# A fused attention and feed-forward kernel: another opening order for its first loads and weights, and other PSUM banks at its end

## The reference

```python
xn = layernorm(x)                                    # over channels, eps 1e-5
q, k, v = (xn @ qkv_w + qkv_b), split into heads
q, k = l2norm(q), l2norm(k)
kv = einsum('bhnd,bhne->bhde', k, v)                 # linear attention: no softmax
att = einsum('bhnd,bhde->bhne', q, kv) @ proj_w + proj_b
ffn = relu(xn @ W1 + b1) @ W2 + b2                   # 1024 inner columns
out = x + att + ffn
```

## Time and profile before

| what | value |
|---|---|
| median of three runs | 557.03 us |
| the profiled execution: its own time | 557.46 us |
| its span, first to last instruction | 555.7 us |
| PE busy | 550.4 us, 99% of the span, 2724 instructions |
| DVE, ACT, POOL busy | 412.8, 285.1, 117.9 us |
| granted TensorE clock | 1.00 in every one of the 40 slices |
| chain that ended last | PE 89%, ACT 3%, DVE 3%, DMA 2% |

### The profile page before, as it was taken

How to read it: one execution, slowest core, us unless ns; L and a number is a source line. 1 busy time by engine, 2 the same in 40 slices (tenths; PEclk the granted TensorE clock), 3 DMA queues, 4 the chain that set the end, 5 groups by cost and what they waited for, 6 DMA issues and landing times.

```text
span 555.7 us, 8968 instructions
## 1 busy us (share of the span) xinstructions
PE 550.4 (99%) x2724; PEld 467.3 (84%) x2724; DVE 412.8 (74%) x802; ACT 285.1 (51%) x518; POOL 117.9 (21%) x148
## 2 busy tenths in 40 slices
PE   9999999999999999999999999999999999999997
PEld 7788888888888888888888888888888888888896
DVE  6897899676795967859677686876778777783755
ACT  4675564656436563365644556455554555533421
POOL 3242424302052020520213202331024301150100
PEclk9999999999999999999999999999999999999999
DMA  8432134343503434134341343414333251313412
GB/s 259 159 87 49 34 83 95 84 103 86 106 14 86 97 87 95 21 85 98 86 87 28 90 95 85 80 37 112 71 94 65 45 106 38 84 32 81 107 39 77
DMA packets 141414, 45.36 MB, mean 82 GB/s; under 512 B 133330, under 2 KB 136402, under 8 KB 141396
## 3 DMA queue, kind: packets, MB, share of 16 engines
q1 hardware_dynamic: 139280, 44.61, 34.8%
q10 hardware_dynamic: 2116, 0.53, 0.5%
HBM read 20.98 MB, written 8.39 MB: 53 GB/s over the span
## 4 chain that ended last, share of the span: by engine, by line
PE 89%; ACT 3%; DVE 3%; DMA 2%; issue 1%; SPq 1%; POOL 0%; DVEq 0%; ACTq 0%; POOLq 0%
PE o_bank L1114 11%; PE o_bank L1113 11%; PE o_bank L1112 11%; PE w_bank L1112 10%; PE w_bank L1113 10%; PE w_bank L1114 10%; PE v_bank L1114 6%; PE v_bank L1113 6%; PE v_bank L1112 6%; PE g_bank L1114 3%; PE g_bank L1113 3%; PE g_bank L1112 3%; DMA w_raw<-w 2%; PE kv_bank L1267 1%; ACT qk_sq L552 0%
## 5 line engine op out<-in xcount | busy, mean ns | idle before, releaser
L574 ACT ACTIVATE h_hi<-w_bank 128x512 fp32r<-128x512 f32 x128 | 76.4, 597 | 66.2 <-PE w_bank L1114 66.0
L908 DVE SCALAR_TENSOR_TENSOR h_lo<-w_bank,h_hi 128x512 fp32r<-128x512 f32 x128 | 87.4, 683 | 28.1 <-ACT h_hi L574 26.4
L1112 PE MATMUL w_bank<-xT_hi,w_hi 128*128 128x512 f32 x254 | 100.1, 394 | 0.4 <-DVE w_lo L743 0.3
L1113 PE MATMUL w_bank<-xT_lo,w_hi 128*128 128x512 f32 x254 | 99.2, 391 | 0.0
L1114 PE MATMUL w_bank<-xT_hi,w_lo 128*128 128x512 f32 x254 | 98.9, 389 | 0.0
L1113 PE MATMUL o_bank<-h_lo,w_hi 128*128 128x512 f32 x240 | 93.4, 389 | 0.0
L1112 PE MATMUL o_bank<-h_hi,w_hi 128*128 128x512 f32 x240 | 93.4, 389 | 0.0
L1114 PE MATMUL o_bank<-h_hi,w_lo 128*128 128x512 f32 x240 | 93.4, 389 | 0.0
L396 POOL TENSOR_TENSOR xn_lo<-xn,xn_hi 128x256 fp32r<-128x256 f32 x56 | 41.5, 742 | 217.9 <-ACT xn_hi L500 213.0
L411 POOL TENSOR_TENSOR y_sb<-y_sb,y_rows 128x256 f32<-128x256 f32 x56 | 53.2, 955 | 124.9 <-DVE y_rows L947 104.3
L552 ACT ACTIVATE qk_sq<-v_bank 128x512 f32<-128x512 f32 x64 | 38.3, 598 | 73.0 <-PE v_bank L1114 71.8
(11 more groups left out here) (205 smaller groups left out, 981.9 us busy)
## 6 DMA issues: line engine op xcount, KB each, us to landing
y_rows<-blocks SPq DMA_DIRECT2D x256, 32.0 KB, 1.9
x_sb<-x SPq DMA_DIRECT2D x15, 512.0 KB, 3.8
y_sb<-x SPq DMA_DIRECT2D x60, 128.0 KB, 3.0
out<-y_sb SPq DMA_DIRECT2D x58, 128.0 KB, 2.5
xT_raw<-blocks SPq DMA_DIRECT2D x224, 32.0 KB, 1.9
y_sb<-w SPq DMA_DIRECT2D x4, 256.0 KB, 4.9
x_sb<-x SPq DMA_DIRECT2D x2, 256.0 KB, 2.9
w_raw<-w SPq DMA_DIRECT2D x2, 256.0 KB, 7.3
```

The source lines that it names most:

```text
L574: nc.scalar.activation(h_hi[:, j % RING, :], w_bank[j % 2][:], ACT.Relu).then_inc(h_done, 1)
L908: nc.vector.scalar_tensor_tensor(h_lo[:, r, :], w_bank[j % 2][:], 0.0, h_hi[:, r, :].bitcast(F32), ALU.max, ALU.subtract).then_inc(h_lo_do ...
L1112: nc.tensor.matmul(to, left[0], right[0], start=first, stop=False, skip_group_check=shared)
L1113: nc.tensor.matmul(to, left[0], right[1], start=False, stop=False, skip_group_check=shared)
```

## The change

Five things, in the words of the program:

1. Loads. SyncE's queue loads x's tiles 0 and 1 as two transfers of 128 KB; tiles 2 and 3 (256 KB) are now issued by ScalarE's queue behind its two small rows. VectorE's statistics wait per tile for the first two.
2. W1's second part. TensorE no longer sums it. `raise_by` writes its spread row into `kv_bank` before the first part's weights are awaited, and so do the spread rows of parts 2 and 3. ScalarE copies the row to SBUF (`second_raise`, in `xn_first`'s place), and GpSimd adds it to the weights once `xn_done` is there. ScalarE and VectorE take high and low from SBUF; VectorE's low part is one instruction of 512 columns instead of two of 256.
3. GpSimd's `w2_low(0)` now waits for W1's first two parts (`w1_ready` 4), `w2_low(1)` for `wqk_raised`.
4. Orders of the opening. ScalarE: W1's part 1 ahead of W2's part 0, W1's part 2 ahead of W2's part 1, `h_high(0, 3)` ahead of the query-key weights. VectorE: `w1_low(2)` ahead of raising the query-key weights, `h_low(0, 3)` ahead of their low part, and `h_low(1, 2)` ahead of `norms(1)`.
5. The end. `attend(b, 0, ...)` of the last batch writes `w_bank[0]` and `v_bank[1]`, and waits for seven of the eight `h_low`.

```diff
-        w1_sum = [v_bank[0], kv_bank]
-        w1_raise = [None, None, g_bank[:, 2 * P:4 * P], v_bank[1][:, 0:2 * P]]
+        last_banks = [w_bank[0], v_bank[1]]
+        w1_sum = v_bank[0]
+        w1_raise = [None, kv_bank[:, 0:2 * P], g_bank[:, 2 * P:4 * P], v_bank[1][:, 0:2 * P]]
+        second_raise = xn_first[:, 0, :]
...
@@ sync
-            for n, loaded in enumerate((x_first_loaded, x_loaded[0])):
-                sp.dma_start(x_sb[:, 0, 2 * n:2 * n + 2, :].rearrange("p e c -> p (e c)"), x_halves[0][:, n]).then_inc(loaded, 16)
+            for t in range(PAIR):
+                sp.dma_start(x_sb[:, 0, t, :], x_halves[0][:, 0, t * C:(t + 1) * C]).then_inc(x_tile_loaded[t], 16)
@@ gpsimd, opening
+                second = part_columns(1)
+                pool.wait_ge(second_raise_copied, 1)
+                pool.wait_ge(w1_loaded[1], 16)
+                pool.wait_ge(xn_done, 1)
+                nc.gpsimd.tensor_tensor(w1_raw[second], w1_raw[second],
+                                        second_raise.unsqueeze(1).to_broadcast([P, KC, 2 * P]), ALU.add).then_inc(w1_second_raised, 1)
+                pool.wait_ge(w1_ready, 4)
                 w2_low(0)
                 pool.wait_ge(qkv_rows_loaded, 32)
                 less_first(slice(0, 2 * C))
+                pool.wait_ge(wqk_raised, 1)
                 w2_low(1)
@@ scalar
+            act.dma_start(x_sb[:, 0, PAIR:TILES, :].rearrange("p e c -> p (e c)"), x_halves[0][:, 1]).then_inc(x_loaded[0], 16)
             act.wait_ge(const_set, 2)
             nc.scalar.activation(unread[:], positive[:], ACT.Sqrt)
             ln_sqrt(0)
+            act.wait_ge(w1_raise_ready, 1)
+            copy(second_raise, w1_raise[1]).then_inc(second_raise_copied, 1)
             w1_high(0)
...
+            w1_high(1)
             w2_high(0)
-            w1_high(1)
...
-                w2_high(1)
                 h_high(0, 2)
                 w1_high(2)
+                w2_high(1)
                 w1_high(3)
+                h_high(0, 3)
@@ vector
+            w1_low(1)
             h_low(0, 0)
-            w1_low_chunk(2)
-            w1_low_chunk(3)
...
                 h_low(0, 2)
+                w1_low(2)
                 dve.wait_ge(qkv_raise_ready, 1)
                 dve.wait_ge(wqk_loaded, 16)
                 raised(wqk_raw, qkv_raise[:, 0:2 * C]).then_inc(wqk_raised, 1)
-                w1_low(2)
+                h_low(0, 3)
                 dve.wait_ge(wqk_hi_ready, 1)
                 less(wqk_lo[:], wqk_raw, wqk_hi[:]).then_inc(wqk_ready, 1)
-                h_low(0, 3)
...
+                h_low(1, 2)
                 norms(1)
                 divide(1, 1, k_done)
-                h_low(1, 2)
@@ tensor
-            for part in range(2):
-                spread_part(part)
-            for part in range(2):
-                raise_part(part)
+            raise_first_part()
             transpose_pair(0)
-            raise_by(w1_raise[2], 4 * P).then_inc(w1_raise_ready, 1)
             transpose_pair(1)
             ffn_up_first()
             ffn_up(0, 0, 1)
-            raise_by(w1_raise[3], 6 * P).then_inc(w1_raise_ready, 1)
...
-                        pe.wait_ge(h_lo_done, JC * (s + 1))
-                        attend(b, 0, w_bank)
+                        pe.wait_ge(h_lo_done, JC * (s + 1) - 1)
+                        attend(b, 0, last_banks)
```

More of the change, by code:

```diff
@@ L154, in build @@
         kv_bank = bank("kv_bank")
+        last_banks = [w_bank[0], v_bank[1]]
         first_banks = [o_bank, [g_bank, kv_bank]]
         pair_banks = [o_bank, [g_bank, w_bank[1]]]
-        w1_sum = [v_bank[0], kv_bank]
-        w1_raise = [None, None, g_bank[:, 2 * P:4 * P], v_bank[1][:, 0:2 * P]]
+        w1_sum = v_bank[0]
+        w1_raise = [None, kv_bank[:, 0:2 * P], g_bank[:, 2 * P:4 * P], v_bank[1][:, 0:2 * P]]
+        second_raise = xn_first[:, 0, :]
         kv_raw = kv_bank[:].rearrange("p (g w n) -> p g w n", g=KC, w=2)
         x_loaded = [sem(f"x_loaded{u}") for u in range(2)]
-        x_first_loaded = sem("x_first_loaded")
+        x_tile_loaded = [sem(f"x_tile_loaded{t}") for t in range(PAIR)]
         y_loaded = [sem(f"y_loaded{u}") for u in range(2)]
@@ L600, in w1_high @@
                 cols = part_columns(part)
-                if part < 2:
-                    act.wait_ge(w1_summed, part + 1)
-                    raised_part = w1_sum[part][:].rearrange("p (k n) -> p k n", k=KC)
+                if part == 0:
+                    act.wait_ge(w1_summed, 1)
+                    raised_part = w1_sum[:].rearrange("p (k n) -> p k n", k=KC)
+                elif part == 1:
+                    act.wait_ge(w1_second_raised, 1)
+                    raised_part = w1_raw[cols]
                 else:
@@ L763, in row_stats @@
                 first = is_first(s)
-                if first:
-                    wait(dve, x_first_loaded, 16)
-                else:
+                if not first:
                     wait(dve, x_loaded[u], 16 * (b + 1))
                 for t in range(TILES):
-                    if first and t == TILES // 2:
-                        wait(dve, x_loaded[0], 16)
+                    if first and t < PAIR:
+                        dve.wait_ge(x_tile_loaded[t], 16)
+                    elif first and t == PAIR:
+                        dve.wait_ge(x_loaded[0], 16)
                     done = nc.vector.bn_stats(ln_parts[:, t, :], x_sb[:, u, t, :])
@@ L825, in raise_w1 @@
             def raise_w1(part):
-                dve.wait_ge(w1_raise_ready, part - 1)
+                dve.wait_ge(w1_raise_ready, part)
                 dve.wait_ge(w1_loaded[part], 16)
@@ L836, in w1_low_chunk @@
                 cols = chunk_columns(j)
-                dve.wait_ge(w1_hi_ready, j // 2 + 1)
-                raised_part = w1_sum[j // 2][:].rearrange("p (k n) -> p k n", k=KC)
-                less(w1_lo[cols], raised_part[chunk_columns(j % 2)], w1_hi[cols]).then_inc(w1_ready, 1)
+                dve.wait_ge(w1_hi_ready, 1)
+                less(w1_lo[cols], w1_sum[:].rearrange("p (k n) -> p k n", k=KC)[cols], w1_hi[cols]).then_inc(w1_ready, 1)
             def transpose_blocks(to, token_major, done):
@@ L935, in add_attention @@
                 to = by_tile(yT[0][:, k, :])
-                nc.vector.tensor_tensor(to, in_pairs((w_bank if last else v_bank)[k][:]), to, ALU.add).then_inc(yT_added, 1)
+                nc.vector.tensor_tensor(to, in_pairs((last_banks if last else v_bank)[k][:]), to, ALU.add).then_inc(yT_added, 1)
             def spread_y(b, u, k):
@@ L1121, in raise_by, with raise_first_part @@
                 return nc.tensor.matmul(to, raise_signs[0:raise_row + 2], raise_rows[:, first:first + to.shape[1]], start=True, stop=True)
[L1123 to L1129, removed]
+            def raise_first_part():
+                sums = [w1_sum[:, k * 2 * P:(k + 1) * 2 * P] for k in range(KC)]
                 for k in range(KC):
-                    nc.tensor.matmul(part_of_sum(part, k), raise_signs[0:raise_row + 2], raise_rows[:, first:first + 2 * P],
+                    nc.tensor.matmul(sums[k], raise_signs[0:raise_row + 2], raise_rows[:, 0:2 * P],
                                      start=k == 0, stop=False, skip_group_check=True)
-            def raise_part(part):
-                first = part * 2 * P
-                pe.wait_ge(w1_loaded[part], 16)
+                for part in range(1, PARTS):
+                    raise_by(w1_raise[part], part * 2 * P).then_inc(w1_raise_ready, 1)
+                pe.wait_ge(w1_loaded[0], 16)
                 for k in range(KC):
-                    done = nc.tensor.matmul(part_of_sum(part, k), ident[:], w1_raw[:, k, first:first + 2 * P],
+                    done = nc.tensor.matmul(sums[k], ident[:], w1_raw[:, k, 0:2 * P],
                                             start=False, stop=k == KC - 1, skip_group_check=True)
```

2 lines of the change are left out of this document (1 added, 1 removed).

## The result

The changed kernel takes 557.95 us (median of 20 runs, 556.62 to 560.24) against 557.03 us (556.40 to 557.87, 20 runs): a ratio of 1.002, 95% interval 1.0012 to 1.0028. It is slower by 0.9 us; forecast was 555.7. The profiled execution took 558.43 us.

A forecast was written before the change was run, and what follows sets the result against it. PE, busy 550.4 of 555.7 us, was taken as the bound. Gains 0.19 + 0.52 + 0.43 + 0.26 = 1.40, less 0.1 for x, gave 1.3 us and a median of 555.7 us, range 555.1 to 556.9.

The forecast's parts named there:

- Part 2: Opening, x's loads: tiles 2 and 3 on ScalarE's queue, taken as 0.1 us later, at most 0.95 us later.
- Rival B: Opening: x's second half shares the engines with W1, lands 0.5 to 0.95 us later; 556.3 us; chance 0.20.
- rival D: Opening: x's second half served only behind W1's four parts; slower, 558.8 us, decided from landing 1.4 us later; chance 0.06.
- I price this at nothing: Ahead of the transposes: TensorE pauses about 0.8 us; clock 1.00 there, so no cost counted.
- part 3: Pause at 18.91 us: W1's part 2 `w_lo` ahead of raising the query-key weights removes it; gain 0.52 us.
- part 4: Pause at 57.16 us: `h_low(1, 2)` ahead of the norms removes it; gain 0.43 us.
- Part 1: Ahead of the transposes: W1's second part no longer summed on TensorE, third `ffn_up` earlier; gain 0.19 us.
- rival C: Pauses move on: PE arrives earlier at `gather` and waits 0.6 us for `k_low`; 556.35 us; chance 0.12.
- Part 5: End, matmul at 543.39 us: `v_bank[1]` for `w_bank[1]` avoids waiting for the last `h_low`; gain 0.26 us.
- GpSimd's price: Opening: GpSimd's addition of 128x512 for W1's second part taken as 1.3 us, from two subtractions of the same size.

The follow-up runs named there:

- experiment 5: Changed kernel with x's loads exactly as before, two of 256 KB on SyncE's queue: 556.60 us [0.9986 to 1.0004].
- experiment 10: Changed kernel with five more warm-up products between W1's first part and the transposes: 557.42 us [0.9998 to 1.0016].
- 1: Changed kernel with x's tiles 2 and 3 issued by SyncE's queue again, behind tiles 0 and 1: 557.06 us [0.9993 to 1.001].
- experiment 2: Kernel before with only x's second 256 KB moved to ScalarE's queue, behind its two rows: 558.32 us [1.0018 to 1.0045].
- 3: Changed kernel with SyncE holding W1's loads back until x's second half is there: 558.12 us [1.001 to 1.0028].
- 4: Changed kernel with ScalarE issuing x's second half ahead of its two rows: 556.71 us [0.9991 to 1.0009].
- 11: Kernel before with x's second half on ScalarE's queue, plus eight more warm-up products ahead of the transposes: 558.76 us [1.0019 to 1.0039].
- experiment 9: Kernel before, unchanged, profiled a second time: 557.54 us.
- 6: Kernel before with only the end's banks changed (`v_bank[1]` for `w_bank[1]`, seven `h_low` awaited for eight): 556.92 us [0.999 to 1.0008].
- 8: Kernel before with the later changed orders, `h_low(1, 2)` ahead of norms and the end's banks; x's loads as before, no raising on GpSimd: 557.14 us [0.999 to 1.0008].
- 7: Changed kernel with x's loads as before and `h_low(1, 2)` behind norms and divide again: 556.73 us [0.9983 to 1.0001].
- Experiment 12: Changed kernel with x's loads as before and VectorE's `m_lo` ahead of the norms' last step in every second half: 556.32 us [0.998 to 0.9998].

## Why the prediction was wrong

The forecast was a gain of 1.3 us; what came was a loss of 0.9. By experiment 5 the loads cost 1.35 us, of it about 0.5 by the clock (experiment 10), for 0.1 in the sum, and all the rest gained 0.46, for 1.40 in the sum.

- **Part 2 failed in size.** I took x's second half 0.1 us late, with 0.95 as the bound; tile 2 was read at 6.22 instead of 4.36, 1.86 us late. Experiments 1 to 5 place it: sharing with W1, which is issued from 1.73 us, 0.1 behind x. The bound failed because I added 256 KB of W1 at the full rate and let the sharing end there, while all four of W1's transfers are issued by 3.70 us, and x lands at 6.2. From 1.50 to 6.25 us the DMA engines moved 252 GB/s (the window under the loads of x), 1.2 MB, of which x is 0.5; so an estimated 0.7 MB of the weights went beside it, where I had allowed 0.26. The Trainium skill ("DMA: Bandwidth & Descriptors", section "Queues, rings and completion order") says that an engine takes turns between queues with work; the runs agree in that the transfer shares: 4.6, 5.9, 3.5 and 4.4 us to land beside W1 (changed, 2, 10, 11), 2.8 us without it (3); that the engines take turns, no run shows. Rival B had the mechanism, rival D the size (beyond its 1.4 us) and the sign; D's extreme, behind all of W1, did not occur.
- **"I price this at nothing" failed.** A wait of TensorE ahead of the transposes let the granted clock fall to 0.50 in experiment 2, and by experiment 10 and the six runs at 0.996 to 0.997 it costs the changed kernel about 0.5 us of its median. That the trace of before showed 1.00 said nothing, since it has no such wait.
- **Parts 3 and 4: the mechanism held, the base did not.** Both pauses went, and against the execution that I read they were worth 0.54 (5, from 13.25 to 20.18 us) and 0.50, for 0.52 and 0.43 forecast. But in experiment 9 and in 6's profile before has no such pauses: a late front fills them. A pause that ends at a fixed time of another chain and what delays PE ahead of it are not two terms of a sum. Against experiment 9, part 3 is worth 0.02 (0.58 and 0.56 gained from 13.25 to 20.18 us), and from 20.18 to 100.08 us the changed kernel loses 0.29 (0.18 gained, and 0.47 by before itself).
- **Part 1, the same error the other way.** From the end of statistics to the third `ffn_up` the changed kernel took 14.66 - 6.97 = 7.69 us, against 12.91 - 5.11 = 7.80: 0.11 for 0.19 forecast. With the late full rate, TensorE's own raising is the bound: experiments 8 and 5 differ by 0.54 in the median, and 8 and 7, whose four spread matmuls both took 1.91 us, by 0.43 at the third `ffn_up` (+0.93 and +0.50 at 13.25). The Trainium skill ("TensorE: Matmul & The Clock Gate", section "What's actually happening") says that the array starts at half its clock, and that the moment of release differs between executions; the traces agree, with 1.03 in one and 1.26 to 1.92 us in the 13 others. I should have asked what the opening is at either rate.
- **Pauses moved on, as in rival C, but elsewhere and for another reason.** Not at `gather`, but at 72 us, where an `ffn_up` follows an `h_low` that has just ended (at 71.97 + 0.69 = 72.66, and PE comes at 72.72), and at 82 us, where the first attention product waits for `m_lo`: together 0.27 to 0.34 us, of which the second is about 0.2. Rival C had PE come earlier; in the changed kernel PE comes 0.64 us later than in the trace read, but `m_lo` 1.08 later (82.44 for 81.36). In 7, with `h_low(1, 2)` back, `m_lo` moves with PE (-0.21 and -0.23 against the trace read); in 5, with the order changed, it does not (-0.80 and -1.21). So the order of part 4 itself sets VectorE back by about 0.4 us against PE, and that eats what it gained at 57 us. Experiment 12 takes the break at 82 away and leaves 0.08 of the other.
- **Part 5 and GpSimd's price held:** 0.26 in the traces of 6 and 5, and 1.29 us for 1.3.

The sum for a usual execution, against experiment 9's profile: front 0.54 later (1.72 - 1.18), 0.07 of it back by 60 us (0.64 - 0.17 = 0.47), the breaks at 72 and 82 us 0.34, the end -0.25: 0.56 us at 546 us. The two spans differ by 0.9, so 0.3 more comes behind that, after PE's last product, and no experiment explains it. In the medians, 14 runs with a clock of 0.998 or more differ from before by 0.37 (557.40), and the six with the lower clock bring that to 0.9.

**Left open.** Whether cutting x's first half into two transfers costs anything: 1 and 5 differ by 0.46 in the median, on two chips, and their intervals overlap. That the clock falls in the opening in the six runs at 0.996 to 0.997 is inferred: only experiment 2's profile shows the fall. It fits in size: 3 us at half rate are 1.5 of 557 us, 0.003 of the mean. How often the full rate comes early in the kernel before; two profiles of it and 6's, with the same opening, show it once in three, and don't give a frequency. Every course above is read from a single profile of its kernel.

## What to carry to other kernels

Before adding up pauses, take a second profile of the same kernel: where two executions with the same total time have different courses, pauses and delays ahead of them cancel, and only what lies on the path in both counts. A load that the first compute waits for belongs ahead of everything else in issue order, on whatever queue: a free queue gave it no share of its own here, and a lead of 0.1 us on W1 did not protect it, one of 0.9 us did. An operand moved forward in an engine's order sets back everything behind it; look for the next wait of the bound engine on that chain too. And a new wait of TensorE, even of 1.4 us, should be priced for the clock.

## What the runs showed of the hardware

- The same 256 KB on the same queue took 2.8 us (only x's other half beside it), 3.2 (issued 0.9 us ahead of W1), and 3.5 to 5.9 (issued behind two rows, 0.1 us ahead of W1 or 0.4 behind it).
- After TensorE's idle stretch of 2.01 us, matmuls ran with the granted clock at 0.50 (1.2 GHz) from 12.5 to 15.5 us; in the runs without a profile, a mean granted clock of 0.996 to 0.997, not 1.00, went with about 2 us more (559.3 to 560.2 for 556.6 to 558.7).
- In the opening the matmuls run at half rate though the clock column has 1.00 for those windows too: in experiment 9 the first four spread matmuls take 1.71 us, and in the trace read, 0.87. Only the lengths of rows show it.
